# Score blocks laid side by side in a PSUM bank, and the expert product over 128 rows, in an eight-batch macaron stack

## What is computed

```python
# mixture of experts: ranks 1, 2, 4, 8, one chosen per token
base = x @ W.T
lw = softmax(logits, axis=1); top1 = argmax(lw, axis=1)
ret = where(arange(E)[None, :] == top1[:, None], lw, 0.0)
res = sum over experts e of ret[:, e] * ((x @ Wd_e.T) @ Wu_e.T)
x = x + 0.5 * (base + res)

# softmax attention: 16 heads of 16, S = 1024 tokens
scores = where(causal, -inf, einsum('bhqd,bhkd->bhqk', q, k) * scale)
out = einsum('bhqk,bhkd->bhqd', softmax(scores, axis=-1), v)
x = x + out @ Wo.T
```

## Time and profile before

| | us |
|---|---|
| median of 3 runs | 3074.97 |
| lowest and highest run | 3060.85, 3075.13 |
| the profiled execution | 3059.91 |
| its span, first to last instruction | 3058.1 |
| PE busy | 2735.0 (89%) |
| DVE busy | 1885.7 (62%) |
| ACT busy | 1213.5 (40%) |
| POOL busy | 749.8 (25%) |

### The profile page before, as it was taken

The page is one execution under the profiler, slowest core; times in us unless marked ns, Lnnn a source line. Parts: engine busy times, 40 slices in busy tenths (PEclk is TensorE's granted clock), DMA queues, the critical chain, the costliest instruction groups (busy, mean ns, idle before and its releaser), DMA issues.

```text
span 3058.1 us, 45977 instructions
## 1 busy us (share of the span) xinstructions
PE 2735.0 (89%) x15374; PEld 1735.1 (57%) x15374; DVE 1885.7 (62%) x5534; ACT 1213.5 (40%) x2706; POOL 749.8 (25%) x1279
## 2 busy tenths in 40 slices
PE   4885899899998999899998999989998999989996
PEld 3663566456655666466655566566664666555544
DVE  5443666665667556666667666675566666666652
ACT  1321244454434444444434343343444444343352
POOL 2321232223222222213322232222322133221111
PEclk7986899999999999899899999999999999999998
DMA  2024103311232213411134112332134111343211
GB/s 58 1 62 112 22 17 95 95 40 40 59 102 74 53 25 95 122 40 39 40 86 123 39 37 61 87 89 52 26 86 120 47 42 36 83 116 78 58 36 45
DMA packets 137424, 193.99 MB, mean 63 GB/s; under 512 B 49439, under 2 KB 111214, under 8 KB 127854
## 3 DMA queue, kind: packets, MB, share of 16 engines
q1 hardware_dynamic: 131808, 190.89, 24.6%
q10 hardware_dynamic: 5390, 0.18, 0.1%
HBM read 122.34 MB, written 67.63 MB: 62 GB/s over the span
## 4 chain that ended last, share of the span: by engine, by line
PE 68%; DVE 15%; DMA 3%; issue 3%; ACT 2%; POOL 1%; SPq 1%; DVEq 0%; ACTq 0%; POOLq 0%
PE bank L735 10%; PE bank L768 8%; PE bank L749 8%; PE bank L664 4%; PE bank L571 4%; PE bank L502 3%; PE bank L551 3%; PE bank L678 3%; PE bank L511 3%; PE bank L520 3%; PE bank L665 3%; DVE bank L1087 3%; DVE mxa L1090 2%; PE bank L481 2%; PE bank L606 2%
## 5 line engine op out<-in xcount | busy, mean ns | idle before, releaser
L1290 ACT ACTIVATE pexp<-bank 128x512 f32<-128x512 f32 (+3 forms) x1536 | 674.7, 495 | 605.3 <-PE bank L749 603.6
L735 PE MATMUL bank<-stk,stq 128*128 128x512 f32 (+3 forms) x1536 | 632.1, 426 | 121.5 <-DVE mxa L1087 33.2
L1087 DVE CUSTOM_DVE_ANT_0 bank<-bank,maskneg 128x128 f32<-128x128 f32 (+3 forms) x1024 | 501.5, 497 | 376.8 <-PE bank L735 371.2
L735 PEld LDWEIGHTS bank<-stk,stq 128*128 128x128 f32 x1536 | 305.4, 201 | 502.1 <-issue 449.7
L749 PE MATMUL bank<-stq,stk 128*128 128x512 f32 (+3 forms) x1536 | 535.6, 422 | 55.3 <-ACT pexp L1290 51.3
L1090 DVE TENSOR_REDUCE mxa<-bank 128x1 f32<-128x512 f32 x512 | 351.8, 687 | 159.7 <-PE bank L735 154.1
L1438 POOL TENSOR_SCALAR_AFFINE_SELECT pexp<-pexp 128x256 f32<-128x256 f32 x512 | 211.6, 419 | 786.9 <-ACT pexp L1290 786.8
L749 PEld LDWEIGHTS bank<-stq,stk 128*128 128x128 f32 x1536 | 281.2, 202 | 196.7 <-ACT pexp L1290 121.6
L768 PE MATMUL bank<-pexp,vsm 128*32 128x512 f32 (+3 forms) x3072 | 360.2, 543 | 8.1 <-POOL pexp L1438 7.7
L1356 POOL TENSOR_SCALAR_AFFINE_SELECT arena<-arena 128x512 f32<-128x512 f32 x128 | 79.4, 644 | 411.2 <-ACT arena L1194 411.2
L571 PE MATMUL bank<-arena 32*128 32x256 f32 x1024 | 155.6, 423 | 15.6 <-DVE arena L895 11.1
(11 more groups left out here) (183 smaller groups left out, 4170.7 us busy)
## 6 DMA issues: line engine op xcount, KB each, us to landing
stq<-q_halves SPq DMA_DIRECT2D x128, 256.0 KB
arena<-rope_table SPq DMA_DIRECT2D x8, 2048.0 KB
q_halves<-arena SPq DMA_DIRECT2D x32, 512.0 KB, 2.9
k_halves<-arena SPq DMA_DIRECT2D x32, 512.0 KB, 2.8
stk<-k_halves SPq DMA_DIRECT2D x64, 256.0 KB
stk<-k_halves SPq DMA_DIRECT2D x128, 128.0 KB
v_rows<-arena SPq DMA_DIRECT2D x16, 544.0 KB, 4.1
vsm<-v_rows SPq DMA_DIRECT2D x16, 544.0 KB, 3.8
```

The lines of the kernel that those rows point to most:

```text
L735: mm(bk[:, 0:k1 - k0], stq[b_][:, h % 2, qb * P:(qb + 1) * P], stk[b_][:, h % 2, k0:k1], start=True, stop=True).then_inc(s["r_full"], 1)
L1087: nc.vector.tensor_tensor_reduce(out=sc, in0=sc, in1=maskneg[:, CH - (k1 - k0):CH], scale=1.0, scalar=LOWEST, op0=ALU.add, op1=ALU.max, ac ...
L1290: nc.scalar.activation(pexp[:, u % NPX, j, 0:n], ps(j)[:, 0:n], ACT.Exp, scale=DK ** -0.5).then_inc(s["exp_done"], 1)
```

## The change

The change has two parts, and some housekeeping.

1. The 12 blocks of a head are put into nine units (`packs`). Three of them hold two blocks side by side in the bank's columns: (qb 0, qb 2), 128 + 384; (qb 1, second part of qb 5), 256 + 256; (second parts of qb 4 and qb 6), 128 + 384. So every unit fills 512 columns. There are 36 units to a group, and `score_at` places three in two core ticks: one at part 0 of the even ones (those that have `values` at part 1), two, at parts 0 and 1, in the odd ones. A unit takes and releases its bank once. Matmuls, reductions and their shapes are the same in number and size.
2. `dg` gets 32 columns for each token tile, 128 in all, with zeros in the 17 unused ones. One transpose of 128 x 128 gives all four tiles below each other. ACT writes, for each tile t, the whole 128 x 128 times the column `tmask[:, t]`, which is one in rows 32t to 32t + 31 and zero elsewhere. The up product then goes over all 128 rows of `dgT[e][:, t]` and `wup`.
3. `tmask` and zeros in `dg` are made once by POOL in the first block (four instructions and two waits); `ktmp` moves into the shared arena.

```diff
-                    for t in range(4):
-                        last = nc.tensor.transpose(bk[0:NR, t * P:(t + 1) * P], dg[:, e, t, 0:NR], ident[:])
-                    last.then_inc(s["f_full"], 1)
+                    nc.tensor.transpose(bk[:, 0:P], dg[:, e].rearrange("p t r -> p (t r)"), ident[:]).then_inc(s["f_full"], 1)
...
-                            last = mm(bk[:, i * D:(i + 1) * D], dgT[e][0:NR, t], wup[0:NR], start=False, stop=True)
+                            last = mm(bk[:, i * D:(i + 1) * D], dgT[e][:, t], wup[:], start=False, stop=True)
...
-                    nc.scalar.copy(dgT[e][0:NR].rearrange("p q c -> p (q c)"), f_bank(q, b, "dgT")[0:NR]).then_inc(f_freed(q, b, "dgT"), 1)
+                    for t in range(4):
+                        last = nc.scalar.activation(dgT[e][:, t], f_bank(q, b, "dgT")[:, 0:P], ACT.Copy, scale=tmask[:, t:t + 1])
+                    last.then_inc(f_freed(q, b, "dgT"), 1)
...
-        sunits = [(h, qb, k0, min(P * (qb + 1), k0 + CH)) for h in range(G) for qb in range(NT)
-                  for k0 in range(0, P * (qb + 1), CH)]
+        packs = (((0, 0), (2, 0)), ((3, 0),), ((1, 0), (5, CH)), ((4, 0),), ((4, CH), (6, CH)), ((5, 0),), ((6, 0),), ((7, 0),),
+                 ((7, CH),))
+        sunits = []
...
-            score_at[SX - LEAD + n // 2, n % 2] = divmod(n, NSU)
-        max_tr_at = {SX - LEAD + NSU // 2 * (g + 1) + 1: g for g in range(NG * NB)}
+            score_at[SX - LEAD + n // 3 * 2 + (n % 3 + 1) // 2, n % 3 // 2] = divmod(n, NSU)
+        max_tr_at = {SX - LEAD + NTU * (g + 1) + 1: g for g in range(NG * NB)}
...
-                    mm(bk[:, 0:k1 - k0], stq[b_][:, h % 2, qb * P:(qb + 1) * P], stk[b_][:, h % 2, k0:k1],
-                       start=True, stop=True).then_inc(s["r_full"], 1)
+                    for qb, k0, n, col in blocks:
+                        last = mm(bk[:, col:col + n], stq[b_][:, h % 2, qb * P:(qb + 1) * P], stk[b_][:, h % 2, k0:k0 + n],
+                                  start=True, stop=True)
+                    last.then_inc(s["r_full"], 1)
```

More of the change, by code:

```diff
@@ L84, in macaron @@
         zcol = sb("zcol", [P, 1])
+        tmask = sb("tmask", [P, 4])
         mhalf = sb("mhalf", [P, NE])
@@ L104, in macaron @@
         krs = sb("krs", [P, 4, H])
-        ktmp = sb("ktmp", [P, 4, H])
         wide = sb("wide", [P, 2, 6, 4 * NE])
         narrow = sb("narrow", [P, 2, 6, 4])
-        dg = sb("dg", [P, 2, 4, NR + 1])
+        dg = sb("dg", [P, 2, 4, HP])
         KB = 256
@@ L135, in macaron @@
         vst = ar(39, 4, H, VP)
+        ktmp = ar(43.25, 4, H)
         projb = [ar(43.5, 4, PROJ), ar(24, 4, PROJ)]
@@ L206, in _ @@
                 nc.gpsimd.memset(zcol[:], 0.0)
+                nc.gpsimd.memset(dg[:], 0.0)
+                nc.gpsimd.memset(tmask[:], 1.0).then_inc(w_tm, 1)
                 nc.gpsimd.memset(vsm[:, :, VW:VW + DK], 0.0)
@@ L215, in select @@
                                                    pattern=pattern, channel_multiplier=cm)
+                pool.wait_ge(w_tm, 1)
+                select(tmask[:], ALU.is_ge, 0.0, 0, [[-HP, 4]], 1).then_inc(w_tm, 1)
                 select(ident[:], ALU.not_equal, 1.0, 0, [[-1, P]], 1).then_inc(w_pool, 1)
@@ L221, in _ @@
                 pool.wait_ge(w_pool, 9)
+                pool.wait_ge(w_tm, 2)
+                select(tmask[:], ALU.is_ge, 0.0, HP - 1, [[HP, 4]], -1)
                 select(hmask[:], ALU.is_ge, 0.0, DK - 1, [[DK, H // KT]], -1).then_inc(w_pool, 1)
@@ L360, in macaron @@
         NTU = len(tunits)
-        sunits = [(h, qb, k0, min(P * (qb + 1), k0 + CH)) for h in range(G) for qb in range(NT)
-                  for k0 in range(0, P * (qb + 1), CH)]
+        packs = (((0, 0), (2, 0)), ((3, 0),), ((1, 0), (5, CH)), ((4, 0),), ((4, CH), (6, CH)), ((5, 0),), ((6, 0),), ((7, 0),),
+                 ((7, CH),))
+        sunits = []
+        for h in range(G):
+            for pack in packs:
+                col, blocks = 0, []
+                for qb, k0 in pack:
+                    n = min(P * (qb + 1), k0 + CH) - k0
+                    blocks.append((qb, k0, n, col))
+                    col += n
+                sunits.append((h, blocks))
         NSU = len(sunits)
@@ L729, in score @@
                 def score(g, i):
-                    h, qb, k0, k1 = sunits[i]
+                    h, blocks = sunits[i]
                     b_ = slot(g, h // 2)
@@ L1081, in core_dve @@
                         g, i = score_at[t, part]
-                        h, qb, k0, k1 = sunits[i]
-                        dst = mxa[:, g % 2, NT * h + qb:NT * h + qb + 1] if k0 == 0 else mxb[:, g % 2, 4 * h + qb - 4:4 * h + qb - 3]
+                        h, blocks = sunits[i]
                         r_filled(nc.vector, "s", g, i)
[L1085 to L1090, removed]
+                        for qb, k0, n, col in blocks:
+                            dst = mxa[:, g % 2, NT * h + qb:NT * h + qb + 1] if k0 == 0 else mxb[:, g % 2, 4 * h + qb - 4:4 * h + qb - 3]
+                            sc = r_bank("s", g, i)[:, col:col + n]
+                            if k0 + n == P * (qb + 1):
+                                last = nc.vector.tensor_tensor_reduce(out=sc, in0=sc, in1=maskneg[:, CH - n:CH], scale=1.0, scalar=LOWEST,
+                                                                      op0=ALU.add, op1=ALU.max, accum_out=dst)
+                            else:
+                                last = nc.vector.reduce_max(dst, sc, AX)
+                        last.then_inc(s["r_used"], 1)
                         if i == NSU - 1:
@@ L1461, in macaron @@
                 for n in range(2 * NG * NB):
-                    at = SX - LEAD + n * NSU // 4 - 4
+                    at = SX - LEAD + n * NTU // 2 - 4
                     if n >= NSLOT:
```

2 lines of the change are left out of this document (1 added, 1 removed).

## The result

The changed kernel takes 2961.91 us in the median of four runs (2955.32 to 2971.39), the kernel before 3070.43 us on the same occasion (3060.85 to 3075.13). The ratio is 0.965, with a 95% interval from 0.961 to 0.969. The forecast was 2986 us with a range of 2935 to 3045 us. So the direction and the range held; of the gain, 108 us, the prediction had found 77.

The account below looks back on a forecast made before the run. PE's work was taken as the bound most of the time. Of 59 us off PE, 50 counted, less 3 for ACT, plus 30 for banks: 77 off 3060 gives 2983; forecast 2986 us, range 2935 to 3045.

Parts of the forecast that it names:

- The bound: PE's work bounds the kernel most of the time; what is taken off it should come off the span.
- The 15-row product: Up product on PE: each of 128 products costs 0.38 us beyond its passes, gone with 128 rows; 49 us.
- The discount of 15%: Of 59 us off PE, 85% counted, since PE also waits elsewhere and DVE-full stretches give part back: 50 us.
- The transposes: dg transposes on PE: three of four go in 32 calls, at 0.106 us each; 10 us.
- The copies: ACT: four 128 x 128 copies replace one of 15 x 512; 7 to 17 us more work, 3 us loss counted.
- The score banks: PE's 101 us of waits for two score banks: about half should lose their cause, 50 us, of which 30 counted.
- no busy time goes: Score units: matmuls and reductions keep number and size, so packing saves only waits and none of the busy time.
- the banks give nothing: Rival on score banks: PE waits for the same DVE work at other lines; 3013 up to 3028 us, chance 0.15.
- the up product gains nothing: Rival on the experts' product: a matmul over 32 rows takes as long as over 128; 3024 us, chance 0.04.
- The burst on DVE: Slower rival: longer odd-tick reductions delay masked products and normalised rows by 0.34 us, 130 us if all exposed; chance 0.08.
- The first rival: Score banks give nearly all waits back, 75 to 101 us: 2923 to 2945 us; chance 0.13 for under 2955.
- The sign of being wrong: Wrong if six passes don't shrink, or PE's batch idle time (23 of 360 us) doesn't fall or outgrows the saving.

Follow-up runs that it names:

- the experiment with 15 rows: Changed kernel with the up product over only the first 15 rows of dgT and wup, transpose and four copies as changed: 3043.5 us, ratio 0.991 to the kernel before.
- the experts alone: Kernel before with only the padded transpose, four masked copies and 128-row up product, scores in 48 units as before: 3006.8 us, ratio 0.979.
- 9.1 in the experiment: Changed kernel with its dg transpose issued four times, only the first result read: 2980.6 us, ratio 0.971 to the kernel before.
- the packs alone: Kernel before with only the packed scores, nine units per head, experts' part as before: 3028.5 us, ratio 0.985.

## Why the prediction was right, and where its sizes were off

**The bound.** Right. PE held the chain and what came off it came off the span: 94 us of busy time, 96 us of span.

**The 15-row product.** The mechanism was right, and it is shown: 1.68 us to 1.29 for six passes, and only with all 128 rows. The count of products and the price of 0.38 us at full clock, 49 us in all, were somewhat high against the 42 us that the ledger gives at full clock from the kernel before to the changed one. What the sum left out was the half clock: another 12 us there, and 31 in the experiment with 15 rows. A product at half clock is dearer (in the trace of before its two passes start 0.59 us apart there, and 0.32 us at full clock), and the number of passes at half clock fell with the change. The discount of 15%, for stretches in which other engines hold PE back, has a counterpart in the ledger: five rows fell by 113 us and the others rose by 15, 13% of it. The times of the experts alone, 64 us against 59 undiscounted, speak against a discount. So this is open.

**The transposes.** 10 us in the sum, 8.0 us in the ledger of the changed kernel, 9.1 in the experiment.

**The copies.** That they are hidden was right, although each takes 0.37 us and not 0.28. The loss of 3 us is neither confirmed nor refuted: three copies fewer gave 3 us, which can't be told from nothing.

**The score banks.** Here the time came out, but not by the mechanism. The step "half of the waits should lose their cause", made from the 101 us of waits, was right in place: the first unit of the odd tick lost its waits, part 0 of even ticks kept them and took over some. As a sum it failed: with the packs alone the waits are still 101 us. And the step "no busy time goes" failed too: PE's busy time fell by 29 us, with the same matmuls, above all at the narrow scores that now stand beside another one. That a term of 30 us, made from waits, lay near the 42 to 47 us of another origin was luck.

**Rivals.** That the banks give nothing fell with the packs alone, that the up product gains nothing fell with the 15 rows. The burst on DVE did not show as a loss: PE's waits for the masked products went from 11.1 to 14.2 us, DVE's load is 63% of the span. The first rival, that the banks give more, had the direction, but its reason, that nearly all waits go, did not come true either. Its sum is also slightly off: with 75 us for the banks it gives 2938 and with 101 it gives 2912, not 2923 to 2945.

**What would show it.** PE's waits at L750 "from 82 us to about 40" was wrong: 66.8. That the remaining ones lie "mostly at part 0 of even ticks" was right: 40.5 of them. "PE busy for 40 to 60 us less" was too low: 94. The sign of being wrong, that the idle time of PE in a batch doesn't fall, was hardly escaped: 23.0 us in the batch from 1100 to 1460 us before, 21.8 in that from 1100 to 1448 after, and 323.1 against 321.3 over the whole span. By that sign the part on the banks was doubtful from the result on.

## What to carry to other kernels

A matmul over part of the rows that stands between full ones had a price at both of its ends here, 0.39 us for each product of 256 columns, alike for 15, 32 and 64 rows; if the operands can be padded with zeros to all 128 rows, with the masking done in a copy that another engine has time for, the price goes. When two engines exchange a small number of banks, fill each bank before it is handed over, and don't set two exchanges directly behind each other. A list of waits is not enough to size such a change: in the packs alone it stayed at 101 us, while the time fell by 42. Sum the distances between starts as well, ask what each row of such a ledger is charged with, and keep those at full and at half clock apart.

## What the runs showed of the hardware

A product over 64 rows is as dear as one over 15: 1.69 and 1.68 us for six passes, against 1.29 with 128. A score of 128 columns is followed by the next start after 0.060 us when the next is another score, and after 0.164 in the median where it stood before, with nothing in the list of waits to show for it. An ACT copy of 128 x 128 from PSUM with a scale taken from a column of SBUF takes 0.368 us in the median, an exponential of the same size with a constant scale 0.277 in the mean. And the price of exchanges directly behind each other was larger than I would have thought: 384 more of them over the run, 12 for each of 32 groups, cost 145 us, 0.38 us for each, while 384 fewer from places apart, with the places changed as well, gave 42 to 47 us, 0.11 to 0.12 for each.
